# Even heads' highs on ScalarE, biases on VectorE, q and k of slots 0 to 7 in f32, new instruction lists

## The reference

```python
x = x + attn(layernorm(x), Wqkv, Wo)      # 16 heads of 32, causal softmax
x = x + ffn(layernorm(x), w1, w3, w2)     # hidden 1365
# attn: a = softmax(where(causal, q @ k.T * 32**-0.5, -1e9)); (a @ v) @ Wo
# ffn:  wq = clip(round(w / mean|w|), -1, 1) * mean|w| for w1, w3, w2
#       (silu(x @ w1q.T) * (x @ w3q.T)) @ w2q.T
```

## Time and profile before

| | us |
|---|---|
| median of 3 runs (lowest, highest) | 583.4 (581.24, 584.58) |
| profiled execution, its own time | 579.74 |
| its span | 578.0 |
| TensorE busy, matmuls | 498.8 (86%), 4092 |
| VectorE busy | 424.9 (74%), 1058 |
| ScalarE busy | 331.5 (57%), 833 |
| GpSimd busy | 370.6 (64%), 461 |

### The profile page before, as it was taken

The page is one execution under the profiler, slowest core; times in us unless marked ns, Lnnn a source line. Parts: engine busy times, 40 slices in busy tenths (PEclk is TensorE's granted clock), DMA queues, the critical chain, the costliest instruction groups (busy, mean ns, idle before and its releaser), DMA issues. The chain is left out here.

```text
span 578.0 us, 11518 instructions
## 1 busy us (share of the span) xinstructions
PE 498.8 (86%) x4092; PEld 230.4 (40%) x4092; DVE 424.9 (74%) x1058; ACT 331.5 (57%) x833; POOL 370.6 (64%) x461
## 2 busy tenths in 40 slices
PE   2658835767997999999999998999999999939997
PEld 2223412232443444544444444444444444414443
DVE  7697878877988798876898986887789883524321
ACT  4878866876765767655357876653477663013320
POOL 3096898866977787865686898673669783322320
PEclk9698975688998999999999999999999999969999
DMA  8729999999689959586568576956583747240001
GB/s 326 266 78 218 180 192 213 207 253 193 132 135 136 182 72 185 75 164 135 137 111 168 93 137 92 199 140 127 92 168 72 144 76 160 80 89 2 0 1 73
DMA packets 224206, 79.52 MB, mean 138 GB/s; under 512 B 213226, under 2 KB 213226, under 8 KB 224148
## 3 DMA queue, kind: packets, MB, share of 16 engines
q1 hardware_dynamic: 224148, 78.79, 66.3%
HBM read 20.97 MB, written 4.19 MB: 44 GB/s over the span
## 5 line engine op out<-in xcount | busy, mean ns | idle before, releaser
L673 POOL TENSOR_TENSOR early<-early 128x512 f16<-128x512 f32 (+1 forms) x192 | 194.7, 1023 | 45.3 <-DVE early L1005 32.2
L781 ACT ACTIVATE early<-early,exp_bias 128x512 f32<-128x512 f32 (+3 forms) x256 | 140.9, 552 | 72.2 <-POOL exp_bias L680 72.1
L1145 PE MATMUL work<-late,w_ternary 128*128 128x512 f16 (+1 forms) x704 | 159.3, 383 | 12.3 <-DMA late<-rows 11.3
L993 DVE CUSTOM_DVE_ANT_0 early<-score_bank,mask,scalars 128x512 f32<-128x512 f32 (+3 forms) x256 | 132.7, 543 | 24.7 <-POOL early L673 16.7
L1005 DVE CAST early<-early 128x512 f16<-128x512 f32 (+1 forms) x148 | 97.8, 675 | 21.7 <-ACT early L781 10.4
L1145 PEld LDWEIGHTS work<-late,w_ternary 128*128 128x128 f16 (+1 forms) x704 | 68.4, 100 | 95.6 <-issue 18.1
L1145 PE MATMUL work<-xt,wqkv_hi 128*128 128x512 f16 x256 | 81.3, 401 | 6.4 <-DMA xt<-rows 4.3
L1308 PE MATMUL work<-w_ternary,late 128*128 128x512 f16 (+1 forms) x352 | 78.1, 379 | 0.2 <-DVE late L1041 0.2
L698 POOL TENSOR_TENSOR late<-late 128x512 f16<-128x512 f32 (+1 forms) x44 | 52.2, 1186 | 37.9 <-ACT late L818 37.0
L811 ACT ACTIVATE late<-work,scalars 128x512 f32<-128x512 f32 (+1 forms) x44 | 29.9, 679 | 40.0 <-PE work L1145 26.3
L1145 PE MATMUL work<-xt,wqkv_lo 128*128 128x512 f16 x128 | 50.8, 397 | 0.0
(11 more groups left out here) (108 smaller groups left out, 718.3 us busy)
## 6 DMA issues: line engine op xcount, KB each, us to landing
rows<-in_L_attn_x SPq DMA_DIRECT2D x16, 256.0 KB, 3.0
x_res<-in_L_attn_x SPq DMA_DIRECT2D x12, 256.0 KB, 3.0
out_y<-x_res SPq DMA_DIRECT2D x12, 256.0 KB, 2.4
late<-in_L_ffn_w SPq DMA_DIRECT2D x4, 682.5 KB, 5.0
early<-in_L_ffn_w SPq DMA_DIRECT2D x3, 768.0 KB, 12.2
late<-in_L_ffn_w SPq DMA_DIRECT2D x3, 768.0 KB, 6.3
late<-in_L_attn_Wqkv SPq DMA_DIRECT2D x4, 512.0 KB, 6.4
late<-in_L_attn_Wqkv SPq DMA_DIRECT2D x1, 1024.0 KB, 9.8
```

What stands on the lines that cost most here:

```text
L673: pool.tensor_tensor(split_view(s, p, 1, h), raw_view(s, p, h), split_view(s, p, 0, h), ALU.subtract).then_inc(low_done, 1)
L781: last = act.activation(piece, piece, ACT.Exp, bias=bias, accum_out=sums[:, s % 2, at:at + 1])
L993: last = dve.tensor_tensor_reduce(raws[n % RAWS][:, off:off + cols], score_bank[h][:, off:off + cols], mask[:, S - cols:S], scalar(exp_sca ...
L1145: last = pe.matmul(bank, lhs, rhs, start=(n == 0), stop=(n == len(terms) - 1))
```

## The change

Four things are changed in the code, and all five lists are laid anew.

- The highs of heads 0 and 2 go to ScalarE in slots 0 to 11, those of heads 1 and 3 stay on VectorE. In slots 12 to 15 ScalarE makes all. It makes 120 in all, VectorE 72.
- The bias, two or four columns wide, is made by VectorE; the function is gone from GpSimd.
- For slots below `WHOLE` = 8, q and k are kept as one f32 tile each (in the bytes that the two f16 halves had), written by ScalarE. There is no low of q and k in these slots, and `scores` does one f32 product per head and tile where three f16 ones stood.
- In TensorE's list, the last slot's second and third fills of scores stand further ahead of their values, and `project:3` stands before `down:2,2-3`. On SP three `res_load` of batch 0 and the first load of w2 stand further ahead.

The code, and of the lists the parts spoken of:

```diff
+WHOLE = 8
...
     "sp": """
-        x_load:1,0-1 weight_load:w3,0-2 weight_turn:w1,1 weight_turn:w1,0 weight_load:w3,3 weight_turn:w1,2
-        probs_turn:0,0-2 res_load:0,3 xt:1,0-1 x_load:1,2 weight_load:w2,0 probs_turn:1,0 x_load:1,3 probs_turn:1,1
+        res_load:0,0 x_load:1,0-1 weight_turn:w1,0 res_load:0,2 weight_turn:w1,1 weight_load:w3,0 res_load:0,3
+        weight_load:w3,1-2 weight_turn:w1,2 weight_load:w3,3 probs_turn:0,0-2 weight_load:w2,0 xt:1,0-1 x_load:1,2
...
     "act": """
+        high:12,1,0 exp:12,1,1-3 high:12,1,1-2 q:14 high:12,1,3 k:15 exp:12,2,0-1 high:12,2,1 v:3,0 high:12,2,0
...
     "dve": """
+        split:2-3 wo_max weight_mean:w1 stats_x:1,0 split:8 max:0,0,0-1 bias:0,0,1 split:4 max:0,0,2 split:5
...
     "pe": """
-        scores:15,0 gate:2,7 lin:2,7 gate:2,8 lin:2,8 scores:15,1 inverse:14 gate:2,9-10 lin:2,9 values:14 lin:2,10
-        scores:15,2 down:2,0-1 inverse:15 down:2,2 values:15 down:2,3 project:3,0-3 gate:3,0-1 lin:3,0-1 gate:3,2-3
+        gate:2,3 values:13 lin:2,3 gate:2,4 scores:14,2 lin:2,4 gate:2,5 scores:15,0 lin:2,5 gate:2,6 lin:2,6
+        scores:15,1 inverse:14 gate:2,7 values:14 lin:2,7 scores:15,2 gate:2,8-9 lin:2,8-9 gate:2,10 lin:2,10
+        inverse:15 down:2,0 values:15 down:2,1 project:3,0-3 down:2,2-3 gate:3,0-1 lin:3,0-1 gate:3,2-3 lin:3,2-3
...
-HALF = numbered("act", "xt", "yt", "q", "k", "v")
+HALF = {step: n for n, step in enumerate(s for s in ORDER["act"] if s[0] in ("xt", "yt", "v") or
+                                         s[0] in ("q", "k") and s[1] >= WHOLE)}
...
-        half = {(n, part_): [sb(f"{n}_{part_}{i}", [P, S], F16) for i in range(HALVES)]
-                for n in "qk" for part_ in ("hi", "lo")}
+        whole = {n: [sb(f"{n}{i}", [P, S], F32) for i in range(HALVES)] for n in "qk"}
+        half = {(n, part_): [w[:, at // 2:(at + S) // 2].bitcast(F16) for w in whole[n]]
+                for n in "qk" for part_, at in (("hi", 0), ("lo", S))}
...
                 full(act, step)
-                act.activation(half[n, "hi"][s % HALVES][:], work[bank_of(step)][:], ACT.Copy,
+                if s < WHOLE:
+                    act.activation(whole[n][s % HALVES][:], work[bank_of(step)][:], ACT.Copy,
+                                   scale=QK_SHRINK).then_inc(work_free[bank_of(step)], 1)
+                    return
...
+            def bias(s, p, h):
+
+                both = slice(piece_columns(p, h - 1).start, piece_columns(p, h).stop)
+                dve.wait_ge(score_free, place(s, p, h) + 1)
+                dve.tensor_scalar(exp_bias[:, (NF * s + p) % 2, both], row_max[:, (NF * s + p) % 2, both], -1.0, LOG_UNIT,
+                                  ALU.mult, ALU.add).then_inc(bias_made, 1)
...
+                at = s % HALVES
+                terms = [(half["q", a][at], half["k", b][at]) for a, b in (("hi", "hi"), ("hi", "lo"), ("lo", "hi"))]
+                if s < WHOLE:
+                    terms = [(whole["q"][at], whole["k"][at])]
                 for j, (tile, off, cols) in enumerate(FILLS[p]):
-                    for t, (a, b) in enumerate((("hi", "hi"), ("hi", "lo"), ("lo", "hi"))):
+                    for t, (q, k) in enumerate(terms):
                         for h in range(HG):
                             if fill and j == t == 0:
                                 pe.wait_ge(score_free, HG * (fill - 1) + h + 1)
                             heads = slice(HD * h, HD * (h + 1))
                             last = pe.matmul(score_bank[h][:, off:off + cols],
-                                             half["q", a][s % HALVES][heads, tile * P:(tile + 1) * P],
-                                             half["k", b][s % HALVES][heads, 0:cols], start=(t == 0), stop=(t == 2))
+                                             q[heads, tile * P:(tile + 1) * P], k[heads, 0:cols],
+                                             start=(t == 0), stop=(t == len(terms) - 1))
```

More of the change, by code:

```diff
@@ L127 @@
[L127 to L131, removed]
+        stats_x:0,0-3 weight_round:w1,0-10 stats_x:1,0 low:0,0,0-3 xt:1,0 low:0,1,0 stats_x:1,1 low:0,1,1-3
@@ new lines @@
+        high:4,0,1 max:4,1,0-1 bias:4,1,1 values:3 high:4,0,3 max:4,1,2-3 bias:4,1,3 v:1,0 high:4,1,1 v:1,1
+        project:0,0 stats_y:0,0 max:4,2,0 high:4,1,3 norm_y:0,0 max:4,2,1-2 project:0,1 bias:4,2,1 project:0,2
+        max:4,2,3 stats_y:0,1-2 v:1,2 norm_y:0,1 high:4,2,1 norm_y:0,2 bias:4,2,3 project:0,3 max:5,0,0 stats_y:0,3
+        high:4,2,3 inverse:4 max:5,0,1 bias:5,0,1 norm_y:0,3 max:5,0,2-3 v:1,3 bias:5,0,3 high:5,0,1 max:5,1,0-1
+        high:5,0,3 bias:5,1,1 max:5,1,2-3 bias:5,1,3 gate:0,0 values:4 lin:0,0 high:5,1,1 stats_x:2,2 max:5,2,0-1
@@ new lines @@
+        bias:7,0,1 max:7,0,2-3 lin:0,8 q:9 high:7,0,1 inverse:6 bias:7,0,3 max:7,1,0 gate:0,9 max:7,1,1 lin:0,9
+        bias:7,1,1 high:7,0,3 gate:0,10 lin:0,10 max:7,1,2-3 high:7,1,1 bias:7,1,3 max:7,2,0 high:7,1,3 values:6
+        max:7,2,1-2 k:9 bias:7,2,1 max:7,2,3 bias:7,2,3 high:7,2,1 q:10 high:7,2,3 down:0,0 max:8,0,0 inverse:7
+        max:8,0,1 bias:8,0,1 down:0,1 max:8,0,2-3 k:10 high:8,0,1 bias:8,0,3 max:8,1,0-1 high:8,0,3 bias:8,1,1
+        values:7 max:8,1,2-3 down:0,2 bias:8,1,3 high:8,1,1 down:0,3 high:8,1,3 max:8,2,0-1 project:1,0 max:8,2,2
@@ new lines @@
+        stats_y:1,0 bias:8,2,1 max:8,2,3 project:1,1 bias:8,2,3 stats_y:1,1 norm_y:1,0 high:8,2,1 max:9,0,0 v:2,0
+        max:9,0,1 high:8,2,3 inverse:8 bias:9,0,1 max:9,0,2 norm_y:1,1 project:1,2 high:9,0,1 max:9,0,3 v:2,1
+        bias:9,0,3 stats_y:1,2 project:1,3 stats_y:1,3 norm_y:1,2 max:9,1,0 norm_y:1,3 max:9,1,1 high:9,0,3
+        bias:9,1,1 v:2,2 max:9,1,2-3 v:2,3 k:11 high:9,1,1 bias:9,1,3 max:9,2,0 q:11 max:9,2,1 gate:1,0 stats_x:3,2
+        bias:9,2,1 values:8 high:9,1,3 lin:1,0 max:9,2,2-3 gate:1,1 lin:1,1 bias:9,2,3 high:9,2,1 max:10,0,0
@@ new lines @@
+        high:11,0,3 max:11,1,0 gate:1,10 max:11,1,1 bias:11,1,1 lin:1,10 max:11,1,2 q:13 values:10 max:11,1,3
+        bias:11,1,3 high:11,1,1 down:1,0 max:11,2,0-1 bias:11,2,1 high:11,1,3 max:11,2,2 high:11,2,1 max:11,2,3
+        bias:11,2,3 max:12,0,0 inverse:11 high:11,2,3 max:12,0,1-2 bias:12,0,1 max:12,0,3 down:1,2 bias:12,0,3
+        down:1,1 max:12,1,0-1 bias:12,1,1 max:12,1,2 down:1,3 values:11 max:12,1,3 bias:12,1,3 max:12,2,0 q:14 k:15
+        max:12,2,1 project:2,0 bias:12,2,1 max:12,2,2 stats_y:2,0 max:12,2,3 project:2,1 bias:12,2,3 stats_y:2,1
@@ new lines @@
+        gate:0,9 lin:0,8-9 scores:7,1 gate:0,10 inverse:6 lin:0,10 k:9 values:6 scores:7,2 down:0,0 q:10 scores:8,0
+        down:0,1 k:10 down:0,2 inverse:7 scores:8,1 values:7 down:0,3 project:1,0 scores:8,2 project:1,1 v:2,0
+        scores:9,0 project:1,2 v:2,1 project:1,3 v:2,2 scores:9,1 v:2,3 k:11 q:11 inverse:8 scores:9,2 gate:1,0
+        values:8 gate:1,1 lin:1,0-1 gate:1,2 scores:10,0 gate:1,3 lin:1,2-3 gate:1,4 inverse:9 gate:1,5 lin:1,4
+        scores:10,1 lin:1,5 gate:1,6 values:9 q:12 gate:1,7 scores:10,2 lin:1,6 k:12 lin:1,7 gate:1,8 scores:11,0
```

293 lines of the change are left out of this document (132 added, 161 removed).

## The result

| | before | after |
|---|---|---|
| median, us | 582.75 (581.24 to 584.58, 4 runs) | 574.97 (572.63 to 576.73, 4 runs) |
| profiled execution, its own time | 579.74 | 574.81 |
| its span | 578.0 | 573.0 |

The ratio is 0.9863, 95% interval 0.9816 to 0.9909: 1.4% faster. A second measurement of the same kernel (`a_again`) gave 0.9882 (0.9843 to 0.9921). The forecast of 573.5 is near, but by large errors that cancel: that is luck.

What follows compares the result with a forecast made beforehand. It took TensorE to bound 184 to 472 us, and a ring of engines, then the DMA queue, the early slots. 579.7 - 8 + 7.4 - 1 - 8 = 570.1, with 3.7 573.8, stated as 573.5; own range 567 to 580, whole 560 to 589.

Steps and rivals of the forecast that it cites:

- The first four slots, 8 us: Attention from 60 to 147 us: shorter hand-overs for biases and highs save 8 us, bounds 0 and 12.
- the trip shrinks by 0.5 to 1.3 of 6.1 us: Early slots: a head's way from maximum to low shortens this much, 7 to 18 of 87 us.
- my own sign of being wrong: The forecast was to count as wrong if the early slots kept their 22 us each.
- the ring: Early slots: four raw buffers make a head's maxima wait for the low four heads before; 18 us a slot.
- f32 scores, 7.4 us: Scores of fills 5,2 to 7,2, uncovered from 184 us on: 3.2 us more a slot, 2.3 slots, 7.4 us lost.
- of each head one record is exposed: f32 scores: one of two records per head uncovered, 4 x 1.3 = 5.2 us a slot, 3.2 more than before.
- The bias, 0.2 us: Each of 96 biases moved to VectorE was taken to cost 0.2 us, 19 us in all.
- The rival: Bias waits for GpSimd: 0.43 us each, VectorE held 22 us more, total 579.8; chance 0.17.
- The bound stretch, 1 us: TensorE's full stretch, 184 to 472 us: fewer waits for lows of q and k save 1 of 4.6 us.
- The end, 8 us: Tail: project ahead of two downs covers the 10.5 us gap; saves 8 of 12.5 us, bounds 0 and 12.5.
- ScalarE falls behind: Last four slots: ScalarE's waits pass 11 us, no end gain, TensorE stalls some 6 us, total 588; chance 0.13.
- the 3.7 that I added: Whole run: the median of the runs, 583.4, stood 3.7 us above the profiled execution, 579.7, so 3.7 was added.

Runs made afterwards that it cites:

- b_bias: Kernel before with only the 96 biases moved from GpSimd to VectorE, each behind its odd head's maximum: 581.74 us against 582.46, ratio 0.9997.
- b_high: Kernel before with only highs moved to ScalarE: even heads' behind their exp, all in slots 12 to 15: 586.85 us against 582.46, ratio 1.0072.
- a_half: Changed kernel with q and k of the first eight slots split into f16 halves again, three score products: 577.97 us, ratio to before 0.9934.
- b_whole: Kernel before with only q and k of slots 0 to 7 whole in f32, one score product for three: 583.1 us against 582.46, ratio 1.0013.
- a_pool_bias: Changed kernel with the 96 biases back on GpSimd: 582.52 us, ratio to before 0.9987.
- b_tail: Kernel before with only down:2,2 and down:2,3 moved behind project:3,3, scores of slot 15 left where they were: 582.31 us, ratio 1.0003.
- a_scores: Changed kernel with scores:15,2 moved back behind gate:2,8 to lin:2,10, its dependent steps likewise: 584.81 us against 582.46, ratio 1.0043.
- a_bias1: Changed kernel with each bias made as one 128x1 operation per column on VectorE instead of one over 2 or 4 columns: 573.42 us, ratio 0.9845.

## Why the prediction came out

**The first four slots, 8 us: failed in its mechanism.** The step was "the trip shrinks by 0.5 to 1.3 of 6.1 us". The mean trip of a head in slots 0 to 3, from the start of its maximum to the end of its low, over 24 even and 24 odd heads (each step's rows taken in the order of the lists):

| us | before | after | `b_bias` | `b_high` |
|---|---|---|---|---|
| pair's last maximum to bias | 0.69 | 0.35 | 0.04 | 0.90 |
| bias | 0.24 | 0.40 | 0.44 | 0.22 |
| bias to the odd exp | 1.52 | 2.52 | 1.54 | 3.17 |
| odd exp to its high | 1.85 | 0.87 | 2.54 | 0.49 |
| whole trip, even, odd | 7.66, 7.96 | 7.47, 7.80 | 7.49, 7.96 | 8.03, 8.21 |

In `a_again` the trip was 7.35 and 7.73. So it shrank by 0.2 to 0.3 us. From scores:0,0 to scores:4,0 it took 99.8 us before, 98.4 after and 96.3 in `a_again`, 25 us a slot and then 24.6 and 24.1: my own sign of being wrong, that the early slots keep their time, came but for 1.4 to 3.5 us.

The premise was thin. I had read the 72.1 us of the earlier trace rows, a sum over the whole run, as what holds this stretch, where it was 20.4; two thirds of that went, and the slots gained little. Nor did VectorE's maxima wait much for the ring to close (1.7 us); its highs waited more, for the transposes of two fills before (7.9) and for exps (6.0). In the changed kernel, the last line, the ring's own wait has grown (all from 60 to 147 us):

```profile
DVE early L1005 <- DMA early<-early: 7.9, 4, 3.6
DVE early L1005 <- ACT early L781: 6.0, 7, 3.1
DVE early L993 <- POOL early L673: 1.7, 5, 0.6
```

```profile
DVE early L990 <- POOL early L675: 9.2, 11, 2.5
```

I had priced the hand-overs that go and not the queue that takes their place. The odd exp waits behind the even high on ScalarE, 1.0 us more; VectorE takes the odd high 1.0 sooner; the bias is picked up 0.34 sooner and is 0.16 longer. Some 3.3 us of the trip are work, the rest is standing in line at engines 70 to 85% busy, and moving a step moves the line. Nor was TensorE saturated before 184 us: from 147 on it was busy 33.7 of 37 us, 33.2 before. Four heads of the changed kernel show these prices (timeline, 92 to 98 us):

```profile
92.22 0.61 ACT L788 ACTIVATE early<-early 128x512 f16<-128x512 f32 x1
...
92.41 0.61 DVE L999 TENSOR_SCALAR exp_bias<-row_max 128x2 f32<-128x2 f32 x1
92.74 0.71 ACT L778 ACTIVATE early<-early,exp_bias 128x512 f32<-128x512 f32 x1
...
96.26 1.15 POOL L683 TENSOR_TENSOR rows<-rows 128x512 f16<-128x512 f32 x1
...
96.90 1.90 DVE L1009 CAST early<-early 128x512 f16<-128x512 f32 x1 [0.23 <-ACT early L778]
97.37 1.15 POOL L675 TENSOR_TENSOR early<-early 128x512 f16<-128x512 f32 x1
```

The odd exp at 92.74 stood behind the even high that ScalarE began at 92.22. VectorE's bias for the next pair takes 0.61 us. Its cast at 96.90, beside two operations of GpSimd, takes 1.90 us where the earlier trace rows had 0.42.

**f32 scores, 7.4 us: a loss, but the term mis-sized.** The step "of each head one record is exposed" failed: the heads do not follow one another; it is 0.84 us a slot, 1.9 in the 2.3 slots. The rule cited from the Trainium skill, "FP8 and Floating Point Precision", section "TensorE Precision Notes" (four passes), gave 0.66 us a slot; the trace's 0.84 is near it. `a_half` and `b_whole` bear out that it is small.

**The bias, 0.2 us: failed.** The rival had 0.43, the trace has 0.48, and of the 19 us foreseen for VectorE 46 came. Its outcome (579.8) did not: by `b_bias` the move costs nothing net on the kernel before, and by `a_pool_bias` taking it back costs about 1% on the changed one.

**The bound stretch, 1 us: right up to gate:2,0** (took less work: 7.8 us before, 7.1 after), **wrong behind it**, 0.6 before and 7.1 after, in slots 14 and 15, where the clock's mean was 0.96 (425 to 468 us).

**The end, 8 us: the right way, 5.6 measured, by other terms.** From gate:2,0 to the end the profile has 8.2 us less, but 2.6 of them are q:15, which only moved ahead of gate:2,0. The gap before the gate shrank by 9.3 us, the values' wait of 0.7 went and 1.9 of clock came back: 11.9, near my upper bound of 12.5. 6.5 were lost ahead of scores:15,2, where I had asked that the engines be faster by 10.6. The reason that I gave first, that project goes ahead of two downs, is not enough: `b_tail` has it and gains nothing, `a_scores` has it and loses. `a_scores` shows that the end follows how early scores:15,2 stands. Whether the early scores need the new place of project as well is not shown, since no run has the one without the other. The rival "ScalarE falls behind" had TensorE stall some 6 us there, and it stood or slowed for 7.1; ScalarE's idle time, 12 of 59 us, just passed the rival's sign of 11. But the waits that the trace names are for VectorE, and the gain was larger than the cost.

The sum forecast -9.6 us; the profiled executions differ by 4.9 (early -0.5, f32 +1.9, bound stretch -0.7, end -5.6) and the medians by 7.8. The early gain was forecast 7.5 too high and the end 2.4; the f32 loss, forecast 5.5 too high, made up for most of that. The rest was made up by the 3.7 that I added for the median over the profile: the changed kernel's profiled execution, 574.81, is within 0.2 of its median. None of this was foreseen, so the nearness of the number bears out no part of the sum. The early share is also the least certain: in `a_again` gate:0,0 came 5.8 us earlier than before, not 0.5, while behind gate:0,0 the two profiles agree (389.6 and 390.3 us, 394.1 before). What lies between 4.9 and 7.8 is within this spread from one execution to the next, below.

Of the parts alone none gains; together, with the lists laid for them, they do. Which share the new order would bring without any part was not tried, so how much of the 1.4% is the parts' and how much the order's stays open.

## What to carry to other kernels

In a ring of engines that are each 70% busy or more, the hand-over that you remove is not the gain: ask who stands in line at the engine that the step moves to, and read the trip, not the link. At a tail, find the step from which a chain of fixed length runs to the end (here 44 us from the last scores to the gate), and count work behind that step; the one swap inside the chain that was tried alone only moved the gap. If a part undone and the same part done alone both lose, the order of the lists is in both measurements, and neither is the price of the part. And a wait summed over a run says nothing of one stretch of it: ask for the stretch.

## What the runs showed of the hardware

- VectorE's bias over 2 or 4 columns takes 0.15 to 1.19 us, one over a single column 0.134 to 0.155, always. In the changed kernel 31 of the 96 ran while GpSimd ran nothing, in 0.15 to 0.17 us each; the 58 that began inside a tensor_tensor of GpSimd had a median of 0.74, and all 43 that took over 0.4 us ended within 0.03 us of the end of a GpSimd operation. Of the 256 single columns (`a_bias1`) 159 began so, and none passed 0.155. The Trainium skill, "GPSIMD Engine Reference", section "1. Specifications", names contention with VectorE's instructions in a 2-port mode or with two SBUF inputs; this would fit if the wider ones are in such a mode and the single column is not. In which mode an instruction ran no trace shows.
- f32 scores make a kernel more open to the clock: fill 0 takes 0.95 us more at half clock, in f16 0.65 (1.47 against 0.82, `a_half`). The f32 fill at half and full clock in one execution:

```profile
85.06 2.09 PE L1232 MATMUL score_bank<-k,q 32*128 32x512 f32 x8 [5.52 <-ACT q L758]
...
113.09 1.14 PE L1232 MATMUL score_bank<-k,q 32*128 32x512 f32 x8
```

In `a_again` TensorE's clock from 60 to 147 us was 0.84 and gate:0,0 came at 178.08; in the first profile of the same kernel it was 0.76 and 183.35. The two were 0.5 us apart at scores:3,0 (113 us) and 3.4 at scores:3,2 (127 us), where their clocks differ; the rest opened behind. That stretch (changed kernel, then `a_again`):

```profile
112.00:130.00 18.00, 17.11 (x155) 8.55 (x154) 11.76 (x48) 14.19 (x38) 11.75 (x14) 0.81 0.92 197
```

```profile
112.00:130.00 18.00, 16.38 (x158) 7.45 (x155) 14.28 (x51) 15.30 (x39) 12.34 (x14) 1.00 1.15 219
```

Over its six runs `a_again` went from 570.14 (mean clock 0.970) to 577.55 (0.959). For this kernel one profiled execution says little about 5 us of the early stretch.
